# Moving the second batch half of a looked-up gated layer into the last turns of a delta-rule loop, and reordering ScalarE in one turn of four

## The chip, the cores and the metric

The kernel runs on one core of a Trainium2 chip. The metric is the device time of one execution in microseconds (us). Before the change the median of three runs is 2019.32 us (2017.99 to 2021.76).

## The reference

The program computes four transformer layers; only the last one is touched. It takes x of 1,024 tokens by 256 features (batch 2 x 512) and adds two branches that both read the same normalised xn:

```python
x = x + _L3_attn_ref(xn, ...) + _L3_ffn_ref(xn, ...)

def _L3_ffn_ref(x, lut, gate_idx, up_idx, down_idx):   # inner width 688
    gate = x @ lut[gate_idx].T
    up = x @ lut[up_idx].T
    return (silu(gate) * up) @ lut[down_idx].T
```

`_L3_attn_ref` is a gated delta rule with 16 key heads and 32 value heads of 128: a projection to q, k, v and z, a causal convolution of four taps with SiLU, per chunk a triangular system that is solved, a state per head that is carried from chunk to chunk, a gated RMS norm and an output projection. All arithmetic is float32.

## The kernel before

Tensors lie transposed: features on the 128 partitions (KC = 2 tiles), tokens along the free dimension, b in {0, 1} for the batch row of T = 512 tokens. The last layer is `delta_and_looked_up`. PSUM is eight banks of 128 x 512, named BG, BK, BT, BO, BW, BZ, BH, BR.

**The loop.** One turn w handles one wave: four chunks at once (PR = 4, two batch rows times two value heads) of 128 tokens. A head has CH = 4 waves, c = w % 4, so there are W = 64 waves, and since the steps of a wave are spread over several turns the loop has W + 2 = 66 turns, 0 to 65. In turn w, TensorE (PE) does for wave w the first joins of the triangular solve (`join_a`, `close_a`, `join_b`), for w-1 the rest of it (`close_b`, `join_c`, `close_c`), the product with the state (`recall`), the solved values (`solve`), the state's growth and the outputs (`grow_state`, `ask`, `answer`), for w-2 the transposes of the normed output (`turn_out`, L2256) and the output projection (`project_out`, L2265), for w+2 the scores (`make_scores`) and turned keys (`turn_keys`), for w+3 the turned values (`turn_values`, L2119). Every engine runs its steps in the order in which they are written in its own loop; the semaphores alone tie them together, and nothing reorders.

**Parts.** The projections of the head after next are cut into twelve parts, `part(w, n)`: three in turns with c = 2 and c = 3, two with c = 0, four with c = 1. PE writes a part into bank BG (n even) or BK (n odd), ScalarE (ACT) copies it out (`copy_raw`, L2416, or `silu_z`, L2420). There are no parts left from turn 58 on. BK also holds the scores. In a turn with c = 0, PE does part 1 after `close_c` (L2195, L2197), but ACT's list has the copy of part 1 before `normed` (L2521, the norm's scale; it frees `turn_out`), `copy_wb` (L2473) and `copy_corners` (L2496, L2497). `exponents(w+3)` (L2442, L2447, L2453) stands ahead of `copy_out` (L2528), for which `project_out` waits; then come `make_keys` (L2464, it frees `turn_values`) and `new_values` (L2503, it frees `answer`).

```python
part(w, 1)
if made(w - 2):
    normed(w - 2)
...
else:
    exponents(w + 3)
if made(w - 2):
    copy_out(w - 2)
```

VectorE (DVE) does the convolutions (`conv(w, 0)` to `conv(w, 3)`, L2686 and L2689), `add_out(w-2)` (L2836), which adds the projected output to x and for which `ask` waits, then `carry` and `gated` (L2797). GpSimd (POOL) runs `substitute(w+2)` on blocks that come back through DRAM, and then `root` (L2649, L2651), which the norm needs. SyncE (SP) issues all DMAs, in its own order, among them `load_t`, which needs the substitution of wave w+1, and, after the loop, eight DMAs of the output (L2052), two for each wave of the last head, each pair as soon as that wave is added.

**The looked-up layer.** Its inner width 688 is cut into WF = 6 tiles (five of 128, one of 48) per batch row: F_TILES = 12. For a tile t, `f_raise` (L2296) makes gate and up: two products of two accumulated matmuls, 128 x 512; `f_silu` (L2533) and `f_mul` (L2845) gate them; `f_lower` (L2306) adds the tile to two banks, and `f_add` (L2852) adds the finished row to x. Tiles 0 to 5 (row 0) are spread among the first steps of the delta rule, where PE has gaps. Tiles 6 to 11 (row 1) run in one stretch ahead of turn 0, and DVE clears two banks (L2928) behind them.

## Time and profile before

| | |
|---|---|
| median of three runs | 2019.32 us |
| the profiled execution's own time | 2018.92 us |
| its span, first to last instruction | 2017.1 us |
| TensorE busy | 1813.0 us (90%) |
| VectorE busy | 1314.6 us (65%) |
| ScalarE busy | 1108.8 us (55%) |
| GpSimd busy | 856.6 us (42%) |
| mean granted TensorE clock | 0.946 of full |

The times below come from the profiled execution and are counted from its first instruction. Turn 0 of the loop begins at 917.33 us and turn 65, the last, at about 2003.3 us. A float32 matmul is two records in the profile (four, for a product accumulated over KC = 2). A record's end is modelled, so the next one starts before it: a group's cost is read from the start of one to the start of the next.

### The profile page before, as it was taken

How to read it: one execution, taken by the hardware profiler on the slowest of the kernel's cores; microseconds unless marked ns; L12 is line 12 of the kernel's file. 1: busy time of each engine (PE TensorE's matmuls, PEld its weight loads, DVE VectorE, ACT ScalarE, POOL GpSimd, SP SyncE). 2: the span in 40 equal slices, each digit the busy share in tenths (PEclk: the TensorE clock that was granted, in tenths of full speed). 3: DMA queues.
4: the chain of work that ended last, by engine and by line, in shares of the span. 5: the costliest groups of instructions: out<-in, count | busy, mean ns of one | idle time of the engine just before them, and what ended most of it. 6: DMA issues, size and time to landing. Idle time of an engine off the chain costs nothing.

```text
span 2017.1 us, 46028 instructions
## 1 busy us (share of the span) xinstructions
PE 1813.0 (90%) x16855; PEld 1181.6 (59%) x16855; DVE 1314.6 (65%) x2778; ACT 1108.8 (55%) x3015; POOL 856.6 (42%) x2131
## 2 busy tenths in 40 slices
PE   7799997877799886898999999999999999999886
PEld 6422564432244565345677777776777677767765
DVE  2544464595669433636787778777877787778652
ACT  2466232224421342535677767776777677777753
POOL 0531122233100241124666666666666665666560
PEclk7999999898999796999999999999999999999988
DMA  5035423110010633112222222222232222222210
GB/s 136 22 95 178 104 46 57 50 64 1 1 44 0 174 116 98 35 24 52 53 52 63 62 52 52 62 58 53 52 63 58 58 53 63 50 62 53 45 37 23
DMA packets 246495, 122.30 MB, mean 61 GB/s; under 512 B 138272, under 2 KB 234016, under 8 KB 246016
## 3 DMA queue, kind: packets, MB, share of 16 engines
q1 hardware_dynamic: 240320, 109.06, 22.8%
q0 software_dynamic: 5952, 10.29, 2.3%
q8 instruction: 137, 2.24, 0.5%
q14 instruction: 86, 0.70, 0.1%
HBM read 87.90 MB, written 37.65 MB: 62 GB/s over the span
## 4 chain that ended last, share of the span: by engine, by line
PE 45%; ACT 8%; issue 2%; POOL 2%; DVE 2%; DMA 1%; SPq 0%; POOLq 0%; ACTq 0%; DVEq 0%
PE ps L2062 10%; PE ps L2072 5%; PE ps L2265 5%; PE ps L2108 3%; PE ps L2239 3%; PE ps L2248 2%; PE ps L2230 2%; PE ps L2296 2%; PE ps L2206 2%; ACT a_xnorm L2521 2%; PE ps L2220 2%; PE ps L2136 1%; PE ps L2147 1%; PE ps L2119 1%; PE ps L2183 1%
## 5 line engine op out<-in xcount | busy, mean ns | idle before, releaser
L2661 POOL TENSOR_TENSOR a_term<-a_z,a_l 32x14 f32<-32x14 f32 (+6 forms) x896 | 295.9, 330 | 70.3
L2665 POOL TENSOR_TENSOR a_z<-a_z,a_term 32x14 f32<-32x14 f32 (+6 forms) x896 | 282.9, 316 | 70.2
L2062 PE MATMUL ps<-all_xn,a_w_qkv 128*128 128x512 f32 x512 | 247.6, 609 | 0.0
L2689 DVE SCALAR_TENSOR_TENSOR a_qkv<-a_raw,a_taps,a_qkv 128x512 f32<-128x512 f32 x300 | 208.3, 750 | 0.0
L2416 ACT ACTIVATE a_raw<-ps 128x512 f32<-128x512 f32 x128 | 78.0, 611 | 126.9 <-PE ps L2062 121.5
L2657 POOL MEMSET a_z<- 32x16 f32 x64 | 7.8, 122 | 323.3 <-DMA a_l<-a_v_dram 323.3
L2265 PE MATMUL ps<-a_out_t,a_w_out 128*128 128x256 f32 x512 | 131.3, 401 | 12.3 <-ACT a_out_t L2528 11.9
L2062 PEld LDWEIGHTS ps<-all_xn,a_w_qkv 128*128 128x128 f32 x512 | 95.1, 193 | 74.7 <-issue 68.0
L2836 DVE TENSOR_TENSOR all_x<-all_x,ps 128x512 f32<-128x512 f32 x64 | 44.0, 688 | 127.2 <-PE ps L2265 127.2
L2072 PE MATMUL ps<-a_w_z,all_xn 128*128 128x256 f32 x512 | 123.9, 385 | 0.0
L2265 PEld LDWEIGHTS ps<-a_out_t,a_w_out 128*128 128x128 f32 x512 | 97.6, 199 | 31.3 <-ACT a_out_t L2528 14.8
L390 POOL DMA_INDIRECT f_rows<-a_row,a_slots x32 | 35.4, 1106 | 184.6 <-DVE a_of_tile L380 139.2
L2740 DVE SCALAR_TENSOR_TENSOR a_v<-ps,a_gates,a_decay 128x128 f32<-128x128 f32 x256 | 72.1, 344 | 54.5 <-PE ps L2108 54.5
L2072 PEld LDWEIGHTS ps<-a_w_z,all_xn 128*128 128x128 f32 x512 | 93.6, 190 | 13.6 <-issue 0.8
L2457 ACT ACTIVATE a_v_row<-ps 128x512 f32<-128x512 f32 x64 | 38.2, 597 | 108.4 <-PE ps L2119 108.4
L850 POOL DMA_INDIRECT f_sums<-a_y,a_xs x23 | 36.1, 1570 | 136.4 <-ACT a_y L799 133.4
L630 PE MATMUL ps<-a_w,a_xt 128*128 x184 | 86.6, 593 | 0.6 <-ACT a_xt L779 0.6
L772 ACT ACTIVATE a_probs<-ps 128x512 f32<-128x512 f32 x128 | 66.1, 602 | 23.8 <-PE ps L593 23.8
L2511 ACT ACTIVATE a_sq<-a_xf 128x128 f32<-128x128 f32 x256 | 75.5, 303 | 4.3 <-DVE a_xf L2797 4.3
L2256 PE MATMUL ps<-a_ident,a_xnorm 128*128 128x128 f32 x256 | 43.2, 296 | 36.2 <-ACT a_xnorm L2521 30.3
L2503 ACT ACTIVATE a_v_new<-ps,a_gates 128x128 f32<-128x128 f32 x256 | 74.3, 394 | 2.2 <-PE ps L2220 2.0
L2725 DVE SCALAR_TENSOR_TENSOR a_low<-a_gc_rows,a_gates,a_floor 128x128 f32<-128x128 f32 x256 | 73.2, 348 | 2.0
(344 smaller groups left out, 4526.5 us busy)
## 6 DMA issues: line engine op xcount, KB each, us to landing
a_gc_rows<-a_g_dram SPq DMA_DIRECT2D x64, 256.0 KB, 4.7
a_v_dram<-a_v SPq DMA_DIRECT2D x64, 256.0 KB, 2.4
a_w<-in_f_w SPq DMA_DIRECT2D x24, 512.0 KB, 4.3
a_w_qkv<-in_a_w SPq DMA_DIRECT2D x16, 512.0 KB, 3.9
a_w_z<-in_a_w SPq DMA_DIRECT2D x16, 256.0 KB, 2.8
a_w_out<-in_a_wo SPq DMA_DIRECT2D x16, 256.0 KB, 2.7
a_v_off<-a_v SPq DMA_DIRECT2D x256, 4.0 KB, 1.8
a_xs<-f_rows SPq DMA_DIRECT2D x25, 130.0 KB, 2.1
```

What stands on the lines that cost most here:

```text
L630: mm = pe.matmul(ps[:, bank + i % 2, :], xt[:, i % 2, k, :], w[:, bass.ds(e, 1), first + k * FF:first + (k + 1) * FF], start=k == 0, stop= ...
L2062: mm = pe.matmul(ps[:, to, :], w_qkv[:, k, mt * P:(mt + 1) * P], xn[:, k, b * T:(b + 1) * T], start=k == 0, stop=k == KC - 1)
L2072: mm = pe.matmul(ps[:, to, i * 256:(i + 1) * 256], xn[:, k, tt * P:(tt + 1) * P], w_z[:, k, :], start=k == 0, stop=k == KC - 1)
L2265: mm = pe.matmul(bank(BO)[:, B * m:B * (m + 1), :], w_out[:, v, m * P:(m + 1) * P], out_t[:, v::VPK, :], start=v == 0, stop=v == VPK - 1)
L2416: act.activation(raw[:, mt, b, TAPS - 1:], ps[:, of, :], ACT.Copy).then_inc(raw_ready, 1)
L2503: act.activation(v_new[:, r, :], bank(BR)[:, r, :], ACT.Copy, scale=gate(K_BETA, w, r)).then_inc(vnew_ready, 1)
L2511: act.activation(sq[:, r, :], xfs[:, w % 2, r, :], ACT.Square, scale=float(P) ** -0.5, accum_out=sums[:, r:r + 1]).then_inc(sq_ready, 1)
L2661: pool.tensor_tensor(term[:, 0:j, j + 1:], z[:, 0:j, j:j + 1].broadcast_to([HP, j, n]), rows[:, j:j + 1, j + 1:].broadcast_to([HP, j, n]), ...
L2665: pool.tensor_tensor(z[:, 0:j, j + 1:], z[:, 0:j, j + 1:], term[:, 0:j, j + 1:], ALU.add).then_inc(sub_step, 1)
L2689: step = dve.scalar_tensor_tensor(to, rows, tap, to, ALU.mult, ALU.add)
L2725: dve.scalar_tensor_tensor(low[:, r, :], gc_rows[:, w % 2, r, :], gate(K_GC, w, r), floor[:, :], ALU.subtract, ALU.min).then_inc(low_ready, 1)
L2740: dve.scalar_tensor_tensor(v0[:, w % 4, r, :], bank(BK)[:, 2 * (r // VPK) + 1, :], gate(K_NBETA, w, r), decay[:, r, :], ALU.mult, ALU.mult ...
```

## The change

It has three parts.

1. The stretch of tiles 6 to 11 ahead of turn 0 is taken out. PE now waits only for row 0's addition, DVE clears the two banks right after the last `silu_z`. The six tiles are computed in turns 60 to 65, one each (`late_tile(w)` = w - 54). `late_raise` puts gate into BG ahead of `turn_keys` and up into BK ahead of `join_b`; `late_silu` follows `copy_out` (and in turn 60 `exponents`); `late_mul` stands ahead of `add_out`; `late_lower` stands ahead of `project_out` and reuses BG and BK; `late_add` adds each tile to x, two instructions per tile, right behind `add_out`. The buffers are those of `raw`, which no head needs any more.
2. The eight DMAs of the output wait for the last of these additions (`f_added` = 14).
3. In all turns with c = 0, ACT copies part 1 after `copy_corners` instead of ahead of `normed`, and `copy_out` goes ahead of `exponents`. On DVE `conv(w, 2)` goes from behind `add_out` to ahead of it.

```diff
+        def late_tile(w):
+
+            t = WF + w - (W + 2 - WF)
+            return t if t >= WF and w < W + 2 else None
...
                 for c in range(CH):
                     sp.wait_ge(added, W - CH + c + 1)
+                    sp.wait_ge(f_added, KC * (F_TILES - WF + 1))
...
+                def late_raise(w, up):
+
+                    t = late_tile(w)
+                    if t is None:
+                        return
+                    f, b, rows = f_tile(t)
+                    if t > WF:
+                        pe.wait_ge(f_added, KC * (t - WF + 1))
+                    if up and made(w + 2):
+                        pe.wait_ge(v0_ready, PR * (w + 3))
+                        pe.wait_ge(far_ready, w + 3)
+                        pe.wait_ge(at_ready, w + 3)
+                    for k in range(KC):
+                        mm = pe.matmul(ps[0:rows, (BG, BK)[up], :], (f_gate, f_up)[up][:, k, f * P:f * P + rows],
+                                       xn[:, k, b * T:(b + 1) * T], start=k == 0, stop=k == KC - 1)
+                    mm.then_inc(up_ready, 1)
+
+                def late_lower(w):
...
+                    pe.wait_ge(gated_ready, t + 1)
+                    for m in range(KC):
+                        mm = pe.matmul(ps[:, (BG, BK)[m], :], f_down[0:rows, f, m * P:(m + 1) * P],
+                                       late_gated[t % 2][0:rows, :], start=True, stop=True)
+                    mm.then_inc(down_done, 1)
...
                 def make_scores(w):
+                    if late_tile(w - 3) is not None:
+                        pe.wait_ge(f_added, KC * (late_tile(w - 3) - WF + 2))
...
-                for t in range(WF, F_TILES):
-                    f_raise(t)
-                    if t > WF:
-                        f_lower(t - 1)
-                f_lower(F_TILES - 1)
+                pe.wait_ge(f_added, KC)
                 pe.wait_ge(cleared, 2)
...
+                def late_silu(w):
...
+                    act.wait_ge(up_ready, 2 * t + 1)
+                    if t >= WF + 2:
+                        act.wait_ge(gated_ready, t - 1)
+                    act.activation(late_act[t % 2][0:rows, :], ps[0:rows, BG, :], ACT.Silu).then_inc(silu_ready, 1)
...
-                    part(w, 1)
+                    if c != 0:
+                        part(w, 1)
...
                     if silus:
                         silu(g, 2)
                         part(w, 2)
+                    if c == 0:
+                        part(w, 1)
+                        if made(w - 2):
+                            copy_out(w - 2)
+                        exponents(w + 3)
                     else:
-                        exponents(w + 3)
-                    if made(w - 2):
-                        copy_out(w - 2)
+                        if not silus:
+                            exponents(w + 3)
+                        if made(w - 2):
+                            copy_out(w - 2)
+                    late_silu(w)
...
-                dve.wait_ge(gated_ready, F_TILES)
+                dve.wait_ge(gated_ready, WF)
+                dve.wait_ge(zs_ready, 4)
                 for n in (BZ, BH):
                     dve.memset(ps[:, n, :], 0.0).then_inc(cleared, 1)
-                f_add(1)
...
                     if c == 2:
                         conv_row(w, 1, 2)
                         conv_row(w, 1, 3)
+                    elif c == 0:
+                        conv(w, 2)
                     if made(w + 2):
                         make_keys(w + 2)
+                    late_mul(w)
                     if made(w - 2):
                         add_out(w - 2)
+                    late_add(w)
                     if c == 0:
-                        conv(w, 2)
                         conv(w, 3)
```

ScalarE in a turn with c = 0 of the loop before, from the copy of part 1 (`a_raw`) to the new values (a_xnorm: `normed`; a_wb, a_inv: `copy_wb`, `copy_corners`; a_decay_far, a_decay, a_grown: `exponents`; a_out_t: `copy_out`; a_k_row: `make_keys`; a_v_new: `new_values`):

```order
L2416 ACTIVATE a_raw<-ps 128x512
L2521 ACTIVATE a_xnorm<-a_xf,a_rstd 128x128 x4
L2473 ACTIVATE a_wb<-ps 128x128
L2496 ACTIVATE a_inv<-ps 64x2x64
L2497 ACTIVATE a_inv<-ps 64x2x64
L2442 ACTIVATE a_decay_far<-a_gc_rows,a_gates 64x64 x2
L2447 ACTIVATE a_decay<-a_low 128x512
L2453 ACTIVATE a_grown<-a_gc_rows 128x512
L2528 ACTIVATE a_out_t<-ps,a_nw 128x512
L2464 ACTIVATE a_k_row<-ps,a_gates 128x128 x4
L2503 ACTIVATE a_v_new<-ps,a_gates 128x128 x4
```

The same turn's ScalarE rows with the change:

```order
L2551 ACTIVATE a_xnorm<-a_xf,a_rstd 128x128 x4
L2503 ACTIVATE a_wb<-ps 128x128
L2526 ACTIVATE a_inv<-ps 64x2x64
L2527 ACTIVATE a_inv<-ps 64x2x64
L2446 ACTIVATE a_raw<-ps 128x512
L2558 ACTIVATE a_out_t<-ps,a_nw 128x512
L2472 ACTIVATE a_decay_far<-a_gc_rows,a_gates 64x64 x2
L2477 ACTIVATE a_decay<-a_low 128x512
L2483 ACTIVATE a_grown<-a_gc_rows 128x512
L2494 ACTIVATE a_k_row<-ps,a_gates 128x128 x4
L2533 ACTIVATE a_v_new<-ps,a_gates 128x128 x4
```

The copy of the part has moved behind four rows, and the copy for the output projection has moved ahead of the exponentials; the keys are still behind them.

ScalarE with the change in turn 60, from `copy_out` on (the second a_raw row is `late_silu`, whose output lies in `raw`):

```order
L2558 ACTIVATE a_out_t<-ps,a_nw 128x512
L2472 ACTIVATE a_decay_far<-a_gc_rows,a_gates 64x64 x2
L2477 ACTIVATE a_decay<-a_low 128x512
L2483 ACTIVATE a_grown<-a_gc_rows 128x512
L2574 ACT_TABLE_LOAD
L2574 ACTIVATE a_raw<-ps 128x512
L2494 ACTIVATE a_k_row<-ps,a_gates 128x128 x4
L2533 ACTIVATE a_v_new<-ps,a_gates 128x128 x4
```

A table load and the SiLU have come in ahead of the keys and the new values; the load appears in turn 60 only.

TensorE with the change in turn 62 (c = 2), from its second late product (`late_raise(62, 1)`; the first stands a few rows ahead, before `close_a`) to `grow_state` (a_raw is the gated tile):

```order
L2098 MATMUL ps<-all_xn,all_looked_up 128x512 x2
L2201 MATMUL ps<-a_tb,a_v 32x32 x8
L2234 MATMUL ps<-a_inv,a_wc 64x64
L2236 MATMUL ps<-a_wc,a_t_half 64x64
L2234 MATMUL ps<-a_inv,a_wc 64x64
L2236 MATMUL ps<-a_wc,a_t_half 64x64
L2245 MATMUL ps<-a_state,a_qkv 128x256 x2
L2295 MATMUL ps<-a_ident,a_xnorm 128x128 x4
L2259 MATMUL ps<-a_rest,a_inv 128x128 x4
L2110 MATMUL ps<-a_raw,all_looked_up 128x512 x2
L2304 MATMUL ps<-a_out_t,a_w_out 128x256 x4
L2287 MATMUL ps<-a_v_new,a_k_row 128x128 x4
```

The L2098 and L2110 rows are new, and the rows between them keep their order. PE reaches the down product (L2110) between `solve` (L2259) and `project_out` (L2304).

## Rows read from the trace of the kernel before

**Rows 1.** Windows (length, engines busy, clock): turn 56; all 14 with c=0

```profile
1869.23:1887.15 17.92, 14.51 (x204) 10.44 (x203) 11.73 (x30) 11.56 (x39) 10.46 (x32) 1.00 0.20 38
sum 253.34, PE 211.50 PEld 153.80 DVE 164.39 ACT 161.75 POOL 157.88; mean PE 15.11 PEld 10.99 DVE 11.74 ACT 11.55 POOL 11.28
```

**Rows 2.** Timeline ahead of turn 0: start, us, engine, line, what, idle before

```profile
883.98 0.60 ACT L2420 ACTIVATE a_zs<-ps 128x512 f32<-128x512 f32 x1 [3.24 <-PE ps L2072]
...
892.36 3.60 PE L2296 MATMUL ps<-all_xn,all_looked_up 128*128 128x512 f32 x8
...
912.44 1.02 DVE L2928 MEMSET ps<- 128x512 f32 x2 [0.18 <-DVE a_rest L2845]
...
916.60 0.28 DVE L2760 TENSOR_TENSOR a_t_wide<-a_t_narrow,a_side 128x128 f32<-128x128 f32 x1
...
917.33 0.65 PE L2136 MATMUL ps<-a_t_wide,a_v_off 32*32 32x32 f32 x32 [1.97 <-issue]
```

**Rows 3.** Timeline of TensorE in turn 56 (c = 0)

```profile
1875.73 1.98 PE L2062 MATMUL ps<-all_xn,a_w_qkv 128*128 128x512 f32 x4
1879.65 0.63 PE L2256 MATMUL ps<-a_ident,a_xnorm 128*128 128x128 f32 x4 [1.94 <-ACT a_xnorm L2521]
...
1882.39 1.99 PE L2265 MATMUL ps<-a_out_t,a_w_out 128*128 128x256 f32 x8 [1.13 <-ACT a_out_t L2528]
...
1885.17 1.16 PE L2230 MATMUL ps<-a_state,a_qg 128*128 128x128 f32 x8 [0.34 <-DVE all_x L2836]
```

**Rows 4.** Timeline of ScalarE in the same turn

```profile
1877.75 0.60 ACT L2416 ACTIVATE a_raw<-ps 128x512 f32<-128x512 f32 x1 [3.44 <-PE ps L2062]
1878.24 1.26 ACT L2521 ACTIVATE a_xnorm<-a_xf,a_rstd 128x128 f32<-128x128 f32 x4
...
1880.02 0.58 ACT L2442 ACTIVATE a_decay_far<-a_gc_rows,a_gates 64x64 f32<-64x64 f32 x2
...
1881.67 0.67 ACT L2528 ACTIVATE a_out_t<-ps,a_nw 128x512 f32<-128x512 f32 x1
```

**Rows 5.** Windows: turn 60, turn 61; sum of turns 61 to 64

```profile
1934.47:1948.26 13.79, 11.17 (x195) 9.04 (x194) 7.67 (x22) 10.31 (x37) 6.82 (x26) 1.00 0.17 33
...
1948.26:1963.68 15.42, 12.09 (x188) 10.36 (x187) 6.86 (x16) 6.55 (x27) 10.54 (x37) 0.78 0.18 38
...
sum 55.04, PE 42.31 PEld 35.69 DVE 18.50 ACT 25.90 POOL 16.36; mean PE 10.58 PEld 8.92 DVE 4.63 ACT 6.47 POOL 4.09
```

**Rows 6.** Timeline of ScalarE ahead of turn 0: keys, then a table load

```profile
869.32 1.14 ACT L2464 ACTIVATE a_k_row<-ps,a_gates 128x128 f32<-128x128 f32 x4
870.48 1.28 ACT L2442 ACT_TABLE_LOAD   x1
```

**Rows 7.** Timeline of TensorE in turn 62 (c = 2)

```profile
1966.06 0.42 PE L2147 MATMUL ps<-a_t_wide,a_wa 32*32 32x32 f32 x29 [1.66 <-ACT a_t_half L2487]
...
1970.24 1.06 PE L2256 MATMUL ps<-a_ident,a_xnorm 128*128 128x128 f32 x4
...
1972.72 1.89 PE L2265 MATMUL ps<-a_out_t,a_w_out 128*128 128x256 f32 x8
```

**Rows 8.** Timeline of turn 65: transposes, output projection, last addition

```profile
2007.70 1.09 PE L2256 MATMUL ps<-a_ident,a_xnorm 128*128 128x128 f32 x4 [4.39 <-DVE a_xnorm L2807]
2009.56 3.56 PE L2265 MATMUL ps<-a_out_t,a_w_out 128*128 128x256 f32 x8 [0.78 <-ACT a_out_t L2528]
2013.16 0.69 DVE L2836 TENSOR_TENSOR all_x<-all_x,ps 128x512 f32<-128x512 f32 x1 [5.61 <-PE ps L2265]
```

**Rows 9.** The output's DMA issues by source line: ns min/median/max, first and last start

```profile
L2052 SPq DMA_DIRECT2D out_t<-all_x x8: 534/621/647, 1975.4 to 2014.5; - x8
```

**Rows 10.** Timeline of GpSimd ahead of turn 0, and in turn 57

```profile
875.89 4.36 POOL L2661 TENSOR_TENSOR a_term<-a_z,a_l 32x14 f32<-32x14 f32 x1
...
1889.62 0.23 POOL L2665 TENSOR_TENSOR a_z<-a_z,a_term 32x14 f32<-32x14 f32 x1
...
1890.95 1.03 POOL L2651 TENSOR_TENSOR a_rstd<-a_var,a_half 128x4 f32<-128x4 f32 x1
```

More of the change, by code:

```diff
@@ L1867, in delta_and_looked_up @@
                    for of in (xfs[:, 0, :, :], xnorm[:, :, :], state[:, :, :], rest[:, :, :])]
+        late_act = [raw[:, n, 0, 0:T] for n in range(2)]
+        late_gated = [raw[:, 2 + n, 0, 0:T] for n in range(2)]
         f_gate = looked_up[:, 0:KC * WIDE].rearrange("p (k n) -> p k n", k=KC)
@@ L2075, in project_z @@
                     mm.then_inc(z_ready, 1)
+                def late_raise(w, up):
[14 more added lines that the diff above has]
+                def late_lower(w):
+                    t = late_tile(w)
+                    if t is None:
+                        return
+                    f, b, rows = f_tile(t)
+                    pe.wait_ge(gated_ready, t + 1)
[3 more added lines that the diff above has]
+                    mm.then_inc(down_done, 1)
                 def part(w, n):
@@ L2373, in _ @@
                     part(w, 0)
+                    late_raise(w, 0)
                     if made(w + 2):
@@ L2397, in _ @@
                     part(w, 3)
+                    late_lower(w)
                     if made(w - 2):
@@ L2534, in f_silu @@
                                    ACT.Silu).then_inc(silu_ready, 1)
+                def late_silu(w):
+                    t = late_tile(w)
+                    if t is None:
+                        return
+                    f, b, rows = f_tile(t)
+                    act.wait_ge(up_ready, 2 * t + 1)
+                    if t >= WF + 2:
+                        act.wait_ge(gated_ready, t - 1)
+                    act.activation(late_act[t % 2][0:rows, :], ps[0:rows, BG, :], ACT.Silu).then_inc(silu_ready, 1)
                 act.wait_ge(small, SMALL * 16)
@@ L2585, in _ @@
                     silu_z(0, n, PROJ[n % 3])
-                for t in range(WF, F_TILES):
-                    f_silu(t)
                 def exponents(w):
@@ L2833, in add_out @@
                     dve.wait_ge(y_psum, w + 1)
+                    if late_tile(w + 1) is not None:
+                        dve.wait_ge(f_added, KC * (late_tile(w + 1) - WF + 2))
                     c = w % CH
@@ L2846, in f_mul, with late_mul, late_add @@
                                       ps[0:rows, f_bank(t, 1), :], ALU.mult).then_inc(gated_ready, 1)
+                def late_mul(w):
+                    t = late_tile(w)
+                    if t is None:
+                        return
+                    f, b, rows = f_tile(t)
+                    dve.wait_ge(up_ready, 2 * t + 2)
+                    dve.wait_ge(silu_ready, t + 1)
+                    if t >= WF + 2:
+                        dve.wait_ge(down_done, t - 1)
+                    dve.tensor_tensor(late_gated[t % 2][0:rows, :], late_act[t % 2][0:rows, :], ps[0:rows, BK, :],
+                                      ALU.mult).then_inc(gated_ready, 1)
+                def late_add(w):
+                    t = late_tile(w)
+                    if t is None:
+                        return
+                    f, b, rows = f_tile(t)
+                    dve.wait_ge(down_done, t + 1)
+                    dve.wait_ge(added, w - 1)
+                    for m in range(KC):
+                        to = x[:, m, b * T:(b + 1) * T]
+                        dve.tensor_tensor(to, to, ps[:, (BG, BK)[m], :], ALU.add).then_inc(f_added, 1)
                 def f_add(b):
@@ L2923, in _ @@
                 f_add(0)
-                for t in range(WF, F_TILES):
-                    f_mul(t)
-                dve.wait_ge(gated_ready, F_TILES)
+                dve.wait_ge(gated_ready, WF)
+                dve.wait_ge(zs_ready, 4)
                 for n in (BZ, BH):
                     dve.memset(ps[:, n, :], 0.0).then_inc(cleared, 1)
-                f_add(1)
                 widen(0)
```

13 lines of the change are left out of this document (3 added, 10 removed).

## The prediction

> **What bounds the kernel now.** I read the windows by turn first, then the timelines inside a turn. In the loop PE sets the pace, and the turns with c = 0 are the exception: turn 56 lasts 17.92 us with PE busy for 14.51 and a granted clock of 1.00, the level of 2.4 GHz [rows 1]. So PE stands for 3.4 us in a turn of which the loop has 14 with work on every step. The timeline names the waits [rows 3]: 1.94 us ahead of the transposes (L2256) for a_xnorm, 1.13 ahead of the output projection (L2265) for a_out_t, 0.34 ahead of L2230 for the addition. ScalarE causes the first two [rows 4]: it idled 3.44 us until PE had made part 1, then copied it at 1877.75, and only behind that scaled xnorm; and a_out_t at 1881.67 stands behind exponentials that began at 1880.02.
>
> Ahead of the loop PE is simply full: eight records of L2296 in 3.60 us, the last of them 0.59 long, are (3.60 - 0.59) / 7 = 0.43 apart [rows 2]. In turns 60 to 65 no projection is left, and PE has gaps: 13.79 us with 11.17 busy in turn 60, 55.04 with 42.31 busy in turns 61 to 64 [rows 5]. There the waits follow one another in a chain of engines, so new work can fill only a gap that stands where it is put.
>
> The measurement of this kernel can tell about 0.2% (4 us) from no change.
>
> **Part 1: the stretch taken out.** After it the loop can begin when silu_z ends, 883.98 + 0.60 = 884.58, plus the clears, 1.02, plus the 0.73 from the widening to the first join (917.33 - 916.60): 886.3 instead of 917.33 [rows 2], or -30.9 us. Row 0's addition is done by then and hides behind silu_z; turn 0's other inputs were ready long before. Bounds -30 and -31.5.
>
> **Part 3: ScalarE in turns with c = 0.** I follow turn 56, which begins at 1869.23, with the new order. PE ends part 1's records at 1875.73 + 4 x 0.43 = 1877.45, and xnorm is ready by 1876, since nothing but the root stands before it: the transposes start there instead of at 1879.65 (-2.2). ACT copies the part at 1877.75 as now, then a_out_t, done at 1878.95 instead of 1882.34: L2265 starts at about 1878.95 instead of 1882.39 (-3.4). The exponentials (1881.67 - 1880.02 = 1.65) now come behind, then the keys (1.14 [rows 6]): 1881.65. PE would want to turn values at 1880.8, so a new wait of 0.85 stands there, on a_k_row. L2230 then starts at 1882.2 instead of 1885.17. The addition has to be there by then: y is ready at 1880.8, and conv(w, 2), now ahead of it, ends at about the same time in a gap of DVE. The turn shortens by 3.0 us; 14 of them give -42. The bounds are -1.9 (the first wait alone, and the second replaced by the wait on the keys) and -3.4 (all gaps): -27 to -48. I take 3.0, because each step of it has its own row. The 14 windows sum to 253.34, against 14 x 17.92 = 250.9 [rows 1], so 2.5 us went to a lower clock that followed the gaps. With shorter gaps most of this should go: -2 (bounds 0 and -2.5). Turns 0 and 60 also have c = 0; turn 0 has no output to project and gains nothing, turn 60 comes below.
>
> **Part 1 again: what the last turns pay.** A tile is 8 + 4 records, 3.4 + 1.7 us of PE. Three more instructions lie in a row with them: SiLU 0.60 (as L2420 [rows 2]), the product 0.69 and two additions of 0.69 each (as L2836 [rows 8]).
> - Turn 60 has c = 0, and its two raises stand where turn 56 has two parts of the same length. So L2265 could start 9.7 us into the turn, as above. But SiLU comes behind the exponentials and needs another table: 1.65 + 1.28 [rows 6] + 0.60 + 0.69 + 1.72 for the down product push it to 15.7. Then 4.4 us as in turn 56 from L2265 to its end, without the 0.34 (1887.15 - 1882.39 - 0.34; the keys are done meanwhile): 20.1 instead of 13.79, +6.3.
> - Turn 62 is the pattern for 61 to 64. PE stood 1.66 us at L2147 and reached the transposes after 6.56 us and L2265 after 9.04 [rows 7]. The first raise covers that wait, the second one of about 0.5, and at the full clock the transposes come at +7.0. Then copy 0.69, SiLU 0.60, product 0.69 and the down product 1.72, with some 0.6 of handing over: L2265 at +11.3, a turn of 15.9. By the same steps turns 61 and 63 take 15.5 and 15.9, and turn 64, whose norm is late anyway, 14.8. Together 62.1 against 55.04 [rows 5]: +7.1.
> - Turn 65: the raises fit into the 4.39 us for a_xnorm [rows 8]. SiLU, product, down product and the two additions add 4.4; transposes and projection, at half clock before (3.56 for L2265, against 1.8), win 2.2: +2.2.
> - The eight DMAs of the output are issued one after another by SP, 0.62 us each [rows 9]. Two followed the last addition; now all eight do: +3.7.
> - This sum of 19.3 is at the full clock. Turn 61 ran at 0.78 of it [rows 5], and turn 60 will have a new hole of nearly 4 us. I add 4, between 0 and 9.
>
> The table load: it starts 0.02 us after the keys end and takes 1.28 [rows 6], and this is what I use. The Trainium skill (ScalarE: Activation LUTs, What ACT_TABLE_LOAD costs) speaks against the new load more strongly: a switch also costs a drain of 1.38 us, 2.66 in all. By that turn 60 would take 1.4 more and the kernel 1.4 more.
>
> **The sum.** -30.9 - 42 - 2 + 19.3 + 4 = -51.6. The profiled execution took 2018.9 us: 1967.3. The median of the runs is 0.4 higher, so I say 1967.
>
> **The rivals.**
> - The second gap of the c = 0 turns stays, as a wait on the keys or on DVE. For it: the keys do stand behind the exponentials. Against it: they end at 1881.65, 2.6 us ahead of the old turning of values. Gain 27 in place of 42: 1982.
> - GpSimd's substitution becomes late. Turn 56's ended at 1889.85, 2.7 us into turn 57, and the root followed (1890.95 + 1.03) [rows 10]. With turn 56 shorter by 3.0 it ends at +5.7, the norm's scale at about +7.1, just when DVE wants it. One GpSimd instruction of 0.2 us took 4.36 while DVE ran convolutions [rows 10]; a second such block costs up to 1 us per head: 1967 + 14 = 1981. The Trainium skill (SBUF — State Buffer, SBUF: two separate sides) has the rule: an instruction of VectorE with two SBUF inputs and one of GpSimd exclude each other for their whole length. The row agrees; the rule would make this rival likelier as DVE's idle time shrinks.
> - More is hidden: the late tiles cost some 12 and the turns with c = 0 give 3.3: 1956.
> - The late tiles run at the low clock, 1.2 instead of 2.4 GHz, for part of the way: 1967 + 20 = 1987.
> - Slower than before: the same, all the way. The chain in turn 60 leaves PE idle, the clock falls and stays down through turns 60 to 65. PE's own work of about 15.5 us per turn (42.31 / 4 = 10.6 [rows 5], a part of it at the low clock, and 5.1 more) would double: 15 x 5.6 = 84, of which 2 per turn falls into waits: +72, 2039. It decides against the change once the lost clock is worth 52 us, that is, low for nearly three quarters of the last turns. Against it: turn 61, with larger gaps, was at 0.78 [rows 5].
>
> That the change doesn't do what it says is excluded for the order: the rows of the instructions show it.
>
> **The numbers.** The forecast gets 0.60; a second gap that stays 0.13; GpSimd 0.10; more hidden 0.10; low clock for a part 0.04; slower 0.03. The range reaches from 1955 (the third rival) to 1985 (the first two, and a part of the unknown clock), which leaves out some 1 in 10 to 2 in 10. Faster: all but the slower rival and a rest of 0.02 at no difference: 0.95, 0.02, 0.03.
>
> **What the profile after would show.** Turn 0 starts at about 886.3. The turns with c = 0 last 14.9 us, PE no longer waits for a_xnorm in them, and a wait of about 0.85 us for a_k_row stands ahead of the turned values. Turn 60 lasts 20 us, with one table load and a hole of nearly 4 us ahead of the down product; turns 61 to 64 together 62. Behind the last addition of x come eight issues in 5 us. I am wrong if the turns with c = 0 keep more than 1.5 us of gaps, if a turn with c = 1 grows, or if turns 60 to 65 show the clock below 0.75.

## The result, and the profile after

| | before | the change |
|---|---|---|
| median | 2020.54 us (four runs beside those of the change) | 1971.73 us (four runs, 1969.10 to 1974.13) |
| ratio | | 0.9755, 95% interval 0.9730 to 0.9779 |
| profiled execution, its own time | 2018.92 us | 1970.71 us |
| span | 2017.1 us | 1968.9 us |
| mean granted TensorE clock | 0.946 | 0.949 |

The forecast was 1967, with a range of 1955 to 1985. The profiled executions differ by 48.2 us, where the forecast had 51.6. The lines of the code have moved: `join_a` is at L2175 now, `turn_out` at L2295, `project_out` at L2304, `turn_values` at L2158, `ask` at L2269, `add_out` at L2884; the new steps are `late_raise` L2098, `late_lower` L2110, `late_silu` L2574, `late_mul` L2905, `late_add` L2917.

The first thing to read is a turn with c = 0. The view is the windows (length, engines busy, clock); the first row is turn 56, the last the sum over all 14 turns of that kind (4, 8, ... 56).

```profile
1796.29:1811.22 14.93, 14.12 (x204) 10.39 (x203) 12.38 (x30) 11.65 (x39) 8.33 (x24) 1.00 0.26 43
sum 208.93, PE 197.56 PEld 145.39 DVE 173.15 ACT 162.95 POOL 119.20; mean PE 14.11 PEld 10.39 DVE 12.37 ACT 11.64 POOL 8.51
```

17.92 us have become 14.93, and the sum has fallen from 253.34 [rows 1] to 208.93, by 44.4. TensorE's timeline of the same turn shows which waits went:

```profile
1804.61 0.60 PE L2295 MATMUL ps<-a_ident,a_xnorm 128*128 128x128 f32 x4
...
1806.04 1.99 PE L2304 MATMUL ps<-a_out_t,a_w_out 128*128 128x256 f32 x8
1808.85 0.66 PE L2158 MATMUL ps<-a_ident,a_qkv 128*128 128x128 f32 x4 [0.81 <-ACT a_k_row L2494]
1809.34 1.06 PE L2269 MATMUL ps<-a_state,a_qg 128*128 128x128 f32 x8
```

The waits of 1.94, 1.13 and 0.34 us [rows 3] are gone. One of 0.81 us for the keys has come ahead of the turned values. ScalarE in that turn, from the copy of part 1 on:

```profile
1804.81 0.60 ACT L2446 ACTIVATE a_raw<-ps 128x512 f32<-128x512 f32 x1 [1.47 <-PE ps L2070]
1805.30 0.68 ACT L2558 ACTIVATE a_out_t<-ps,a_nw 128x512 f32<-128x512 f32 x1
1806.01 0.58 ACT L2472 ACTIVATE a_decay_far<-a_gc_rows,a_gates 64x64 f32<-64x64 f32 x2
...
1807.67 1.12 ACT L2494 ACTIVATE a_k_row<-ps,a_gates 128x128 f32<-128x128 f32 x4
```

Now the start of the loop, in the timeline of all engines (compare [rows 2]):

```profile
881.64 0.60 ACT L2450 ACTIVATE a_zs<-ps 128x512 f32<-128x512 f32 x1 [3.24 <-PE ps L2080]
...
882.83 1.02 DVE L2998 MEMSET ps<- 128x512 f32 x2 [1.83 <-ACT a_zs L2450]
...
884.67 0.65 PE L2175 MATMUL ps<-a_t_wide,a_v_off 32*32 32x32 f32 x32 [3.08 <-DVE a_t_wide L2813]
```

The stretch is gone, and the loop begins 32.7 us sooner. Of that 2.3 us are not the change's: `silu_z` ended at 882.24, not 884.58. (In the kernels run later that have no stretch either, and the same program up to there, turn 0 began between 881.71 and 886.48.) Then the last turns, again as windows: turn 60; turns 61 to 64 as one; turn 65 up to the first output transfer.

```profile
1858.54:1881.37 22.83, 18.36 (x208) 12.28 (x207) 9.68 (x25) 12.56 (x39) 11.22 (x42) 0.85 0.10 20
1881.37:1945.05 63.68, 58.91 (x700) 40.27 (x699) 26.07 (x62) 28.26 (x110) 12.34 (x37) 1.00 0.06 13
1945.05:1961.59 16.54, 11.50 (x25) 4.91 (x24) 4.04 (x6) 2.44 (x10) 1.25 (x2) 0.79 0.00 0
```

Turn 60 has the predicted hole, and the granted clock falls in it. First ScalarE there, then TensorE:

```profile
1867.45 0.69 ACT L2558 ACTIVATE a_out_t<-ps,a_nw 128x512 f32<-128x512 f32 x1
...
1869.30 0.61 ACT L2483 ACTIVATE a_grown<-a_gc_rows 128x512 f32<-128x512 f32 x1
1869.93 1.28 ACT L2574 ACT_TABLE_LOAD   x1
1871.22 0.60 ACT L2574 ACTIVATE a_raw<-ps 128x512 f32<-128x512 f32 x1
```

```profile
1872.67 3.78 PE L2110 MATMUL ps<-a_raw,all_looked_up 128*128 128x512 f32 x4 [4.09 <-DVE a_raw L2905]
1876.24 2.36 PE L2304 MATMUL ps<-a_out_t,a_w_out 128*128 128x256 f32 x8
```

`project_out` had its operand at 1868.14 and ran at 1876.24, since it stands behind the down product in TensorE's list. Two more windows hold the stretches of turns 60 and 65 in which the granted clock was 0.50, that is 1.2 of 2.4 GHz:

```profile
1870.36:1877.19 6.83, 4.52 (x7) 2.28 (x8) 0.69 (x1) 3.51 (x10) 4.52 (x18) 0.50 0.00 0
1952.28:1959.11 6.83, 6.83 (x12) 3.47 (x12) 0.00 (x0) 0.00 (x0) 0.00 (x0) 0.50 0.00 0
```

The first begins inside the hole (1868.58 to 1872.67), so TensorE worked in only 4.52 of its 6.83 us; in the second it worked all the time. Last, turn 65 and the output:

```profile
1949.50 0.63 PE L2295 MATMUL ps<-a_ident,a_xnorm 128*128 128x128 f32 x4 [0.82 <-DVE a_xnorm L2853]
...
1952.16 3.69 PE L2110 MATMUL ps<-a_raw,all_looked_up 48*128 48x512 f32 x4 [2.03 <-DVE a_raw L2905]
...
1955.78 3.62 PE L2304 MATMUL ps<-a_out_t,a_w_out 128*128 128x256 f32 x8
1959.44 0.69 DVE L2884 TENSOR_TENSOR all_x<-all_x,ps 128x512 f32<-128x512 f32 x1 [7.33 <-PE ps L2304]
1960.23 1.29 DVE L2917 TENSOR_TENSOR all_x<-all_x,ps 128x512 f32<-128x512 f32 x2
1961.59 5.29 SPq L2060 DMA_DIRECT2D out_t<-all_x  x8
```

The whole account, each term from these two traces:

| | forecast | measured |
|---|---|---|
| start of turn 0 | -30.9 | -32.7 |
| 14 turns with c = 0, clock included | -44 | -44.4 |
| all other turns up to turn 60 | 0 | +1.1 |
| turn 60 | +6.3 | +9.0 |
| turns 61 to 64 | +7.1 | +8.6 |
| turn 65 up to its last addition | +2.2 | +5.9 |
| from there to the end (transfers) | +3.7 | +4.1 |
| low clock, in no turn in particular | +4 | in the rows above |
| sum | -51.6 | -48.2 (the rows add to -48.4; the 0.2 is rounding) |

### The profile page after: what moved, and what is told of

Its sections match the earlier page's. It is cut to its first block, busy times and chain, and to the rows that moved or that the text cites. A ratio compares the mean times of both kernels' runs of the same rounds, so it can differ in the third digit from the quotient of the medians.

```text
span 1968.9 us, 46060 instructions
## 1 busy us (share of the span) xinstructions
PE 1799.2 (91%) x16855; PEld 1171.4 (59%) x16855; DVE 1322.8 (67%) x2788; ACT 1109.4 (56%) x3016; POOL 857.5 (44%) x2131
## 4 chain that ended last, share of the span: by engine, by line
PE 46%; ACT 7%; issue 2%; DVE 1%; POOL 1%; DMA 1%; SPq 0%; ACTq 0%; POOLq 0%; DVEq 0%
PE ps L2070 10%; PE ps L2080 6%; PE ps L2304 3%; PE ps L2147 3%; PE ps L2278 3%; PE ps L2287 3%; PE ps L2269 2%; PE ps L2245 2%; PE ps L2158 2%; PE ps L2259 1%; ACT a_k_row L2494 1%; PE ps L2175 1%; PE ps L2186 1%; PE ps L2222 1%; ACT a_decay L2477 1%
## 5 line engine op out<-in xcount | busy, mean ns | idle before, releaser
L2711 POOL TENSOR_TENSOR a_z<-a_z,a_term 32x14 f32<-32x14 f32 (+6 forms) x896 | 292.1, 326 | 70.2
L2707 POOL TENSOR_TENSOR a_term<-a_z,a_l 32x14 f32<-32x14 f32 (+6 forms) x896 | 282.8, 316 | 70.3
L2304 PE MATMUL ps<-a_out_t,a_w_out 128*128 128x256 f32 x512 | 127.2, 392 | 0.6 <-ACT a_out_t L2558 0.6
L2304 PEld LDWEIGHTS ps<-a_out_t,a_w_out 128*128 128x128 f32 x512 | 95.1, 193 | 21.2 <-issue 5.4
L2884 DVE TENSOR_TENSOR all_x<-all_x,ps 128x512 f32<-128x512 f32 x64 | 44.0, 687 | 58.3 <-PE ps L2304 58.1
L2697 POOL TENSOR_TENSOR a_rstd<-a_var,a_half 128x4 f32<-128x4 f32 x64 | 73.0, 1140 | 5.3
L2456 ACT ACTIVATE a_qkv<-a_qkv 128x1024 f32<-128x1024 f32 x64 | 67.5, 1055 | 13.3 <-DVE a_qkv L2735 13.3
```

The source lines that it names most:

```text
L2304: mm = pe.matmul(bank(BO)[:, B * m:B * (m + 1), :], w_out[:, v, m * P:(m + 1) * P], out_t[:, v::VPK, :], start=v == 0, stop=v == VPK - 1)
L2697: pool.tensor_tensor(rstd[:, :], var[:, :], half[:, :], ALU.pow).then_inc(rstd_ready, 1)
L2707: pool.tensor_tensor(term[:, 0:j, j + 1:], z[:, 0:j, j:j + 1].broadcast_to([HP, j, n]), rows[:, j:j + 1, j + 1:].broadcast_to([HP, j, n]), ...
L2711: pool.tensor_tensor(z[:, 0:j, j + 1:], z[:, 0:j, j + 1:], term[:, 0:j, j + 1:], ALU.add).then_inc(sub_step, 1)
```

## The experiments

Ten kernels were run, in three groups, each group beside its own runs of the kernel before (medians 2022.13, 2018.97 and 2025.17 us). Since those medians move by some us from group to group, kernels of different groups are compared by their ratios to before, or inside their traces.

### Which of the parts brings the gain: the order, or the tiles?

**e1**: the kernel before, with part 3 of the change alone.

```diff
-                    part(w, 1)
+                    if c != 0:
+                        part(w, 1)
...
-                        exponents(w + 3)
-                    if made(w - 2):
-                        copy_out(w - 2)
+                        if not silus:
+                            exponents(w + 3)
+                        if made(w - 2):
+                            copy_out(w - 2)
```

(with the new branch for c = 0, and `conv(w, 2)` ahead of `add_out`, as in the change)

> The kernel before with the third part of the change alone (ScalarE's order and DVE's conv(w, 2) in turns with c = 0; tiles 6 to 11 stay ahead of turn 0). Theory: the two parts don't touch one another, and the 14 turns with c = 0 last 14.9 us as in the changed kernel: -44 us, of which 2.5 from the clock, so about 1975. Rival: the order pays only together with the tiles moved (DVE and ScalarE free in between): turns of 16 to 17 us, about 2000.

Measured: 1975.00 us, ratio 0.9755 (0.9724 to 0.9786), the ratio of the whole change.

**e2**: the changed kernel with part 3 undone.

```diff
-                    if c == 0:
-                        part(w, 1)
-                        if made(w - 2):
-                            copy_out(w - 2)
-                        exponents(w + 3)
-                    else:
-                        if not silus:
-                            exponents(w + 3)
-                        if made(w - 2):
-                            copy_out(w - 2)
+                    else:
+                        exponents(w + 3)
+                    if made(w - 2):
+                        copy_out(w - 2)
```

(the copy of part 1 and `conv(w, 2)` also go back to their old places)

> The changed kernel with the old order of ScalarE and DVE in turns with c = 0 (the tiles alone are moved). Theory: ahead of the loop -30, at the end +28, turns 0 to 3 +1: -1 to -4 against before, about 2017; that is, moving the tiles gains next to nothing by itself. Rival: the two parts help one another and the tiles alone lose, +5 or more. In turn 60 SiLU comes ahead of neither: exponents, copy, SiLU, as long as now.

Measured: 2019.06 us, ratio 0.9979 (0.9961 to 0.9997). Windows of e1 first: the sum of its 14 turns with c = 0.

```profile
sum 209.54, PE 197.83 PEld 145.43 DVE 173.22 ACT 162.79 POOL 123.93; mean PE 14.13 PEld 10.39 DVE 12.37 ACT 11.63 POOL 8.85
```

And windows of e2: turn 56, everything from turn 60 to the end, and the sum of the 14 turns.

```profile
1839.59:1857.51 17.92, 14.50 (x203) 10.44 (x203) 11.72 (x30) 11.56 (x39) 10.72 (x33) 1.00 0.22 39
...
1904.61:2013.70 109.09, 87.86 (x929) 57.04 (x928) 39.80 (x93) 43.32 (x159) 25.50 (x82) 0.92 0.09 22
...
sum 254.89, PE 215.78 PEld 157.42 DVE 164.28 ACT 161.76 POOL 154.54; mean PE 15.41 PEld 11.24 DVE 11.73 ACT 11.55 POOL 11.04
```

The reordering is nearly the whole gain: the 14 turns take 209.54 (e1) and 208.93 (the change) with it, 254.89 without it. Moving the six tiles buys 32.4 us at the start of the loop (884.88 against 917.33) and pays 26.5 at the end: from turn 60 on e2 takes 109.09, the kernel before takes 82.63, as the next row, its own, shows.

```profile
1934.47:2017.10 82.63, 58.14 (x857) 47.99 (x856) 28.25 (x75) 38.18 (x152) 24.43 (x78) 0.87 0.12 28
```

The turns between, 0 to 59, take 2.6 more. What is left of the tiles' move in e2's trace is 3.4 us, and e2's runs agree (0.9979 is some 4 us). By the ratios the change has 0.9755 and the order alone also 0.9755, so once the order is in, the tiles' move adds nothing that the runs tell from zero. Their intervals leave room for some 8 us either way; the two profiled spans are 1974.7 (e1) and 1968.9.

### Which piece of the order brings it?

**e3**: the changed kernel, with the exponentials ahead of `copy_out` again where c = 0.

```diff
                         part(w, 1)
+                        exponents(w + 3)
                         if made(w - 2):
                             copy_out(w - 2)
-                        exponents(w + 3)
```

> The changed kernel with the exponentials ahead of the copy for the output projection again in turns with c = 0, the rest as changed. Theory: the second gap comes back in part, project_out starts 1.65 us later, the wait on the keys (0.85) goes: turns of 15.7 to 15.8, +12 us. Rival: the keys bound the turn either way: 14.9, no difference.

Measured: 1989.76 us, ratio 0.9834 (0.9812 to 0.9856). The turns with c = 0 take 16.28 us each. TensorE's timeline of turn 56 in e3:

```profile
1822.24 1.06 PE L2259 MATMUL ps<-a_rest,a_inv 128*128 128x128 f32 x8
1825.01 1.99 PE L2304 MATMUL ps<-a_out_t,a_w_out 128*128 128x256 f32 x8 [1.71 <-ACT a_out_t L2558]
...
1827.78 1.16 PE L2269 MATMUL ps<-a_state,a_qg 128*128 128x128 f32 x8 [0.34 <-DVE all_x L2884]
```

So of the 3.0 us per turn, moving the copy of the part behind the norm brings 1.64 (17.92 to 16.28), and moving `copy_out` ahead of the exponentials 1.35. The wait is at another place: 1.71 us for a_out_t and 0.34 for the addition, where the change has 0.81 for the keys. I had expected turns of 15.7 to 15.8 and +12 us; the wait for the addition came back too, which I had left out, and 14 times 1.35 is 18.9.

**e4**: the changed kernel, with `conv(w, 2)` behind `add_out` again.

```diff
-                    elif c == 0:
-                        conv(w, 2)
...
                     if c == 0:
+                        conv(w, 2)
                         conv(w, 3)
```

> The changed kernel with conv(w, 2) behind add_out again in turns with c = 0. Theory: DVE has the time on either side, no difference within 1.5 us. Rival: two convolutions in a row delay gated and with it the next turn: 0.3 to 1 us per turn, +4 to +14.

Measured: 1970.07 us, ratio 0.9737 (0.9709 to 0.9765), its turns with c = 0 as long as the change's, 14.93. Moving the convolution does nothing that can be measured.

### What the last turns pay for

From turn 60 to the end the change takes 110.36 us, against 82.63 before.

```profile
1858.54:1968.90 110.36, 88.77 (x929) 57.46 (x928) 39.79 (x93) 43.26 (x159) 24.81 (x81) 0.91 0.09 21
```

Is that the tiles' own work, or the chain of copy, SiLU, product and down product that now stands ahead of each output projection?

**e5**: the changed kernel, with the down product behind the projection.

```diff
-                    late_lower(w)
                     if made(w - 2):
                         project_out(w - 2)
+                    late_lower(w)
```

> The changed kernel with one move: in the late turns the late tile's down product stands behind the turn's output projection on TensorE, no longer ahead of it. My theory: the late tile is dear because its down product waits for copy_out, SiLU and product while the projection, whose operand is there earlier, stands behind it, and because the clock falls behind that hole. Then turn 60 takes about 20 to 21 us instead of 22.8, turns 61 to 64 about 1 us less each, turn 65 about 8.5 instead of 16.5 up to its last addition: 8 to 10 us below the change in all, about 1963. Rival: the late tile costs what its matrix products and its second addition take, wherever they stand: no more than 2 us below the change, about 1970.

Measured: 1956.44 us, ratio 0.9700 (0.9665 to 0.9735). Windows of e5: turn 60; all from turn 60 on; turns 61 to 64; turn 65.

```profile
1855.54:1875.46 19.92, 17.52 (x207) 12.36 (x206) 9.55 (x25) 12.69 (x39) 12.28 (x43) 0.91 0.12 23
...
1855.54:1952.80 97.26, 82.80 (x929) 55.67 (x928) 39.80 (x93) 43.43 (x159) 26.03 (x82) 0.95 0.10 24
1875.46:1934.32 58.86, 57.11 (x699) 39.89 (x698) 26.21 (x62) 28.29 (x110) 12.50 (x37) 1.00 0.07 14
1934.32:1945.50 11.18, 8.17 (x25) 3.42 (x24) 4.04 (x6) 2.44 (x10) 1.25 (x2) 1.00 0.00 0
```

The end is 13.1 us shorter (97.26 against 110.36) with the same 929 matmul records: 2.9 in turn 60, 4.8 in turns 61 to 64, 5.4 in turn 65, where the clock stays at 1.00. My theory holds, and I had put its worth too low in all (8 to 10 us), though too high in turn 65, which I expected at 8.5 and which took 11.2. Nearly half of what the tiles' move costs at the end was the place of one step, not its work.

**e6**: as e5, and in turn 60 ScalarE does the late SiLU right behind `copy_out`; the exponentials of wave 63 come last.

```diff
                         if made(w - 2):
                             copy_out(w - 2)
-                        exponents(w + 3)
+                        if not late:
+                            exponents(w + 3)
...
                         part(w, 2)
+                        if late:
+                            exponents(w + 3)
```

(`late` is true in the turns that have a late tile)

> As e5, and in turn 60 ScalarE does the late SiLU right behind copy_out and the exponentials of the next wave last, as in the turns 61 to 64. My theory: what makes turn 60 the dearest is the five exponentials and the table load ahead of the SiLU; with them behind it turn 60 takes 16.5 to 17.5 us, its hole of 4 us on TensorE and the low clock behind it are gone, and the kernel ends 3 to 5 us below e5, at 1958 to 1961. There is one table load more. Rival: with the down product already behind the projection the exponentials no longer hold TensorE up, and moving them puts the wait on the next wave's scores: within 1.5 us of e5.

Measured: 1954.27 us, ratio 0.9668 (0.9627 to 0.9708). ScalarE in its turn 60, windows of turns 60 and 61 behind it:

```profile
1869.69 1.28 ACT L2574 ACT_TABLE_LOAD   x1
1870.98 0.60 ACT L2574 ACTIVATE a_raw<-ps 128x512 f32<-128x512 f32 x1
...
1873.66 1.28 ACT L2472 ACT_TABLE_LOAD   x1
```

```profile
1860.08:1876.57 16.49, 15.87 (x208) 11.10 (x208) 9.55 (x25) 13.11 (x39) 10.14 (x37) 1.00 0.14 27
1876.57:1891.85 15.28, 14.60 (x199) 9.94 (x199) 8.46 (x19) 9.10 (x31) 7.58 (x28) 1.00 0.22 47
```

Turn 60 takes 16.49 us at the full clock, as expected, 3.4 less than in e5. There are two more table loads than in e5 (here and in turn 61, 1.28 us each), where I had expected one. Turn 61 is 0.9 longer than in e5: its load stands ahead of its SiLU, and TensorE waits 0.58 us there for the gated tile, where in e5 it waits for nothing. From turn 60 to the end the trace gives 94.72, 2.5 below e5. The medians differ by 2.2, and the intervals overlap: the trace shows the hole closed, the runs alone don't separate the two kernels.

**e7**: the changed kernel with other output transfers: row 0's in eight pieces as its waves are added, row 1's in two of 256 KB behind the last addition of a tile.

```diff
                     sp.wait_ge(added, W - CH + c + 1)
-                    sp.wait_ge(f_added, KC * (F_TILES - WF + 1))
                     for k in range(KC):
-                        to = d["out_t"][k * P:(k + 1) * P, :].rearrange("p (b t) -> p b t", b=B)
-                        of = x[:, k, :].rearrange("p (b t) -> p b t", b=B)
-                        sp.dma_start(to[:, :, c * P:(c + 1) * P], of[:, :, c * P:(c + 1) * P]).then_inc(stored, 16)
+                        sp.dma_start(d["out_t"][k * P:(k + 1) * P, c * P:(c + 1) * P],
+                                     x[:, k, c * P:(c + 1) * P]).then_inc(stored, 16)
+                sp.wait_ge(f_added, KC * (F_TILES - WF + 1))
-                sp.wait_ge(stored, 16 * CH * KC)
+                for k in range(KC):
+                    sp.dma_start(d["out_t"][k * P:(k + 1) * P, T:], x[:, k, T:]).then_inc(stored, 16)
+                sp.wait_ge(stored, 16 * (CH * KC + KC))
```

> The changed kernel with its output transfers rearranged: those of batch row 0, which is complete sooner, are issued while the last waves run, and behind the last addition stand only two of row 1, of 256 KB each, in place of eight. My theory: the tail behind the last addition is the issue of many transfers one behind the other and the time of the last; it is 7.4 us in the change and was 3.3 before, and comes to 4 to 4.5: 3 us below the change, about 1968.5. Rival: a transfer of 256 KB takes as much longer to land as the issues save: no difference, 1971.5.

Measured: 1964.78 us, ratio 0.9732 (0.9687 to 0.9777). Its timeline at the end:

```profile
1956.19 1.28 DVE L2918 TENSOR_TENSOR all_x<-all_x,ps 128x512 f32<-128x512 f32 x2
...
1957.50 0.81 SPq L2061 DMA_DIRECT2D out_t<-all_x  x2
```

The additions end at 1957.47, the span at 1960.6: a tail of 3.1 us against 7.4. The tail's 4.2 us are in the trace. The whole span is 8.3 us shorter than the change's (1960.6 against 1968.9): besides the tail, turn 0 is 3.3 shorter at a higher clock (see the last section) and turn 60 is 0.5 shorter. The interval of its ratio takes in the change's 0.9755, so the runs alone don't separate these two.

**e8**: as e6, with the tiles in turns 59 to 64.

```diff
-            t = WF + w - (W + 2 - WF)
-            return t if t >= WF and w < W + 2 else None
+            t = WF + w - (W + 1 - WF)
+            return t if WF <= t < F_TILES else None
```

> As e6, and the six late tiles go into the turns 59 to 64 in place of 60 to 65, so that nothing of them is left behind the last wave. My theory: in turn 65 there is no next wave's work that would cover the late tile's chain of copy_out, SiLU and product, so the tile costs its whole chain there and about 2.5 us in turn 59, whose other work covers it: the tail goes back to that of the kernel before (turn 65 about 10.6 us, 3.3 us behind the last addition), 8 to 10 us of the end's 16, less 2.5: 3 to 5 us below e6, about 1955. Rival: with the down product behind the projection (e5) turn 65's tile is already cheap, and turn 59 pays as much: within 1.5 us of e6.

Measured: 1954.76 us, ratio 0.9685 (0.9651 to 0.9719), not to be told from e6. From turn 59 on e8 takes 107.67 us and e6 109.84, by their windows:

```profile
1844.63:1952.30 107.67, 94.93 (x1131) 64.97 (x1130) 48.87 (x121) 58.64 (x199) 33.52 (x112) 0.96 0.11 26
```

```profile
1844.96:1954.80 109.84, 94.42 (x1131) 65.56 (x1130) 48.85 (x121) 55.64 (x197) 32.73 (x110) 0.95 0.11 25
```

The tail behind the last addition falls from 7.3 to 3.2 us, but turn 59 grows from 15.1 to 17.4, and turn 65 hardly shrinks (10.5 for 11.1): without a tile it is a chain in which TensorE waits 4.39 us for a_xnorm and then runs `project_out` at the low clock, 3.78 us where e5 needed 1.99. Here the rival was right: with the down product in its better place the last tile was cheap already.

**e9** (e8 with e7's transfers) and **e10** (e9, and where c = 0 the exponentials behind the keys and the new values) close the study. The edit of e10 on e9:

```diff
                             copy_out(w - 2)
-                        if not late:
-                            exponents(w + 3)
...
                     if made(w - 1):
                         new_values(w - 1)
+                    if c == 0 and not late:
+                        exponents(w + 3)
```

> The two edits that helped apart, together: the late tiles in the turns 59 to 64 with their down product behind the output projection (e8), and the output transfers of row 0 issued early (e7). With the last tile in turn 64, what stands behind the last addition is short in either form: two transfers of 64 to 256 KB. My theory: the transfers of e7 gained because eight issues stood behind the last addition; in e8 the additions of the late tiles end a turn before the end, six of the eight issues are already under way then, so little is left to gain: 0 to 1.5 us below e8, about 1954. Rival: the two edits add up, since the last transfers are what counts: 3 us below e8.

Measured: 1954.00 us over five runs, ratio 0.9657 (0.9635 to 0.9678): within the noise of e8, so the runs don't tell the theory (0 to 1.5 us below e8) from the rival (3 us). The traces do: behind the last addition stand 4.1 us in e9 and 3.2 in e8, so the transfers of e7 gain nothing there. That e9's span is still 2.3 us shorter (1950.0 against 1952.3) comes from turn 0, 12.66 us for 15.58.

> As e9, and in the turns with c = 0 ScalarE does the keys and the new values ahead of the exponentials of the wave after next, which then stand last. My theory: of the 0.8 us for which TensorE still stands in such a turn, all is the wait for a_k_row behind the exponentials; it goes, and the addition at about 1808.8 in a turn that reaches the state's product at 1808.5 puts back 0.2 to 0.3: these turns take 14.3 to 14.4 us instead of 14.93, 14 of them 7 to 9 us, so 1946. Rival: the exponentials, now 3 us later, are late for VectorE's decayed scores in the next turn or hold up the copy of the turned values, and the turns with c = 0 or c = 1 are as long as before or longer: 1954 or more.

Measured: 1949.85 us over five runs (1947.68 to 1950.96), ratio 0.9637 (0.9615 to 0.9659). Its turn 56: the window, TensorE, and ScalarE.

```profile
1790.28:1804.78 14.50, 14.16 (x203) 10.49 (x202) 12.35 (x30) 11.64 (x39) 7.89 (x22) 1.00 0.16 31
```

```profile
1802.81 1.16 PE L2270 MATMUL ps<-a_state,a_qg 128*128 128x128 f32 x8 [0.34 <-DVE all_x L2889]
```

```profile
1799.87 1.14 ACT L2495 ACTIVATE a_k_row<-ps,a_gates 128x128 f32<-128x128 f32 x4
...
1802.06 0.58 ACT L2473 ACTIVATE a_decay_far<-a_gc_rows,a_gates 64x64 f32<-64x64 f32 x2
```

The wait for the keys was caused by the exponentials: with those behind, it is gone, and 0.34 us for the addition stands in its place. The turn lasts 14.50 us, not the 14.3 to 14.4 I expected, so 14 turns give 6.0. The medians of e9 and e10, run side by side, differ by only 4.15, and the spans by 4.1: in its trace e10 begins the loop 0.95 us later, and its turn 2 takes 19.27 us where e9's takes 18.10. So some of the 6.0 is missing at the start of the loop; why was not tried. The gain over e9 is clear of the noise (e10's highest run is 1950.96, e9's lowest 1951.84), and by the ratios e10 is below the change (0.9659 at most, against 0.9730 at least).

## Why the prediction was right, step by step

- **ScalarE in turns with c = 0.** Forecast 3.0 us per turn and a new wait of 0.85 on a_k_row; measured 2.99 and 0.81. e1 shows that this part alone is the gain. The step assumed that the addition would be ready in time, and it was: nothing waits for it in the change. The share of each piece was not forecast; e3 gives 1.64 and 1.35. That `conv(w, 2)` ahead of `add_out` matters was never claimed, and e4 shows that it doesn't.
- **The clock of these turns.** Forecast -2 us; the sum of the 14 rows is 208.93, which is 14 times 14.92, so nothing is lost to a low clock any more. e2, with the old waits, loses it: 254.89 against 14 x 17.92 = 250.9.
- **The stretch ahead of turn 0.** Forecast -30.9 (its own terms, 917.33 - 886.33, give -31.0); measured -32.7, of which 2.3 came from work upstream that the change does not touch. That is -30.3 for the step itself.
- **Turn 60.** Forecast 20.1 us at the full clock; measured 22.83 at 0.85. From 1870.36 to 1877.19 the granted clock was at its lower level, 1.2 of 2.4 GHz. The first 2.3 us of that lie in the hole, where a low clock costs nothing; of the 4.52 in which TensorE worked half is lost, 2.3. The rest of the 2.7 above the forecast is the wait of 0.34 for the addition, which I had taken out and which stayed, and 0.15 by which the down product started later than forecast. The hole was 4.09 where I had said nearly 4. The table load took 1.28 us, right behind the last exponential (1869.30 + 0.61, then 1869.93) and with SiLU right behind it. There is no drain of 1.38 in the row beside it, nor beside the two loads of e6 that are shown (the second ends at 1874.94, and the next activation starts at 1874.95); for the kernel before, the row that I took the price from [rows 6] has none either. The Trainium skill (ScalarE: Activation LUTs, What ACT_TABLE_LOAD costs) adds one, and here the row decides.
- **Turns 61 to 64.** Forecast +7.1, measured +8.6: the pattern of turn 62, 15.9 us, came out at 16.35. Its transposes came at +7.24 instead of +7.0 and the projection at +11.70 instead of +11.3.
- **Turn 65: the term that was mis-sized.** I had the transposes and the projection win 2.2 us because they would leave the low clock, and costed the down product at the full clock. The transposes did (0.63 for 1.09), the projection did not: behind the chain's wait of 2.03 us the granted clock was low from 1952.28 to 1959.11, the down product took 3.69 instead of 1.7 and the projection 3.62 instead of 1.8. Together 3.8 us, and the turn came out 3.7 above the forecast (+5.9 for +2.2). e5 shows that it is the place of the down product: with it behind the projection, TensorE waits only 0.83 and 0.78 us in this turn, the clock stays at 1.00, and projection and down product take 1.99 and 1.98. It is no chance of one execution: the change, e2, e3, e4 and e7, which have the old place, each have 6.83 us of low clock in turn 65, and e5 and e6, which have the new one, none.
- **The output.** Forecast +3.7, measured +4.1, and e7 takes these 4.2 us back.
- **The low clock.** I had +4 for all last turns; the trace shows 2.3 in turn 60 and 3.4 in turn 65 (half of 6.83), the latter inside the term above.

**The rivals.** A second gap that stays did not come, though e3 makes nearly that kernel, and its ratio, 0.9834, would put it at some 1986 here against the rival's 1982. GpSimd did not become late. The turn behind turn 56 took 16.54 us before (first row, kernel before) and 16.52 in the change (second row), with TensorE busy all the time in both (the 14 turns with c = 1, from turn 5 to turn 57, add to 231.2 us before and 231.3 in the change):

```profile
1887.15:1903.69 16.54, 16.54 (x227) 14.29 (x227) 14.29 (x32) 15.37 (x37) 9.73 (x29) 1.00 0.20 44
```

```profile
1811.22:1827.74 16.52, 16.52 (x224) 14.27 (x223) 13.71 (x30) 15.27 (x37) 11.05 (x34) 1.00 0.21 46
```

So the Trainium skill's rule on VectorE and GpSimd (SBUF — State Buffer, SBUF: two separate sides) cost this change nothing. The instruction of 4.36 us [rows 10] agrees with it, but the turns with c = 1 were not on GpSimd's path even after 3 us of slack had gone. More was not hidden: the end costs 27.7 us, more than the 23.3 of the forecast, and the turns with c = 0 gave 2.99 each, not 3.3. A low clock for part of the late tiles did come, but at 5.7 us (2.3 and 3.4) instead of that rival's 20. The slower case, a clock that stays low through all last turns, did not come: turns 61 to 64 had 1.00.

**What the forecast did not see** is how the two big parts relate. It had -42 and -2 for the order, and -11.6 (-30.9 + 19.3) for the tiles before the clock; the tiles' move brought 3.4 us alone (e2), because the end costs 26.5, or 27.7 in the change itself, instead of 23.3 with the clock, and turns 0 to 59 cost 2.6 where I had nothing.

**How near the total came is partly luck.** Turns 60 to 65 lie 7.9 us above their terms (2.7, 1.5 and 3.7). The 4 us set aside for the clock cover half of that, and 2.3 us from work upstream, which no term foresaw, another part. The mechanism of the 14 turns, which is the gain, needed no luck.

## What to carry to other kernels

In an engine's hand-written list, a step that waits holds up every step behind it, so look first at what stands *behind* the waiting one: here a copy for later use ahead of a norm, and exponentials for the wave after next ahead of a copy needed at once, cost 3 us in every fourth turn. When work moves into gaps, put the step at the end of its chain behind the steps of the turn that are ready sooner (e5: 13 us of 28), and count what it pulls with it, such as all transfers of the output. A move that seems to win 30 us where it leaves may give nearly all of them back where it arrives.

## What the runs showed of the hardware that was not expected

- **What a hole costs in clock differs from one execution to the next, and only the part that falls on work counts.** Turn 60's hole of 4.09 us is in the change and in e7, whose program is the same there. In the change the clock was low for 6.83 us, 4.52 of them with TensorE at work: 2.3 lost. In e7 it was low from 1870.37 to 1873.78, all of it work: 1.7 lost. So turn 60 took 22.83 us at 0.85 and 22.29 at 0.92. In e5 a hole of 2.36 us was followed by 3.41 us of low clock as well (19.92 us at 0.91), 1.7 lost; e6, with a hole of 0.58, has none.
- **Turn 0 differs by more than most edits are worth, for a reason that is open.** The change and e7 have the same program up to there, yet turn 0 took 15.55 us at 0.72 in one and 12.30 at 0.99 in the other. The rows, the change first, then e7:

```profile
884.67:900.22 15.55, 10.40 (x122) 5.84 (x123) 9.98 (x24) 5.79 (x13) 4.82 (x11) 0.72 0.29 70
```

```profile
885.55:897.85 12.30, 7.15 (x122) 4.10 (x122) 10.12 (x24) 5.78 (x13) 3.59 (x10) 0.99 0.30 58
```

  This difference follows one edit: turn 0 took 12.30 and 12.66 us in e7 and e9, which have e7's transfers (and 9.13 in e10, which has them and does its keys sooner), and 15.45 to 15.70 in the change and the other seven. In those eight the clock was low as turn 0 began; in the three it was not. But that edit changes only what SyncE does after the loop, and each kernel has one trace, so they don't show whether it is cause or chance. It is a reason to compare stretches of the traces and not only medians. What in the work ahead of turn 0 decides its clock was not tried.
